# One core: the first step written out apart, odd experts' weights a step later, two reorderings at layer one's opening and tail, and the first pair's down projection a step nearer

## The chip, the core and the metric

The kernel runs on one core of one Trainium2 chip, in one launch. The core's engines run their own instruction lists side by side and meet at semaphores: PE (TensorE, matrix products and transposes), DVE (VectorE), ACT (ScalarE), POOL (GpSimd) and SP (SyncE, which here only issues DMAs). The metric is the device time of one launch in microseconds (us), the median of several runs.

## The reference

Eight sequences of 1024 tokens of 128 features go through a sparse feed-forward layer, a linear attention and the same feed-forward layer again:

```
x = x + 0.5 * ffn(layernorm(x))
x = x + attn(layernorm(x))        # elu+1 features, 16 heads of 8, kv = k^T v, then q kv
x = x + 0.5 * ffn(layernorm(x))
...
logits = xf @ gate_w + gate_b                       # 16 experts
top_vals, top_idx = top_k(softmax(logits), 2)       # two experts a token
y = sum over the two of  w * ((silu(x @ w1 + b1) * (x @ w3 + b3)) @ w2 + b2)
z = (silu(x @ sw1 + sb1) * (x @ sw3 + sb3)) @ sw2 + sb2     # shared, inner width 352
ffn = y + z
```

## The kernel before

There are 64 tiles of 128 tokens, in 8 groups of 8 tiles (a group is one sequence) and 16 chunks of 4 tiles. Five phases follow each other, with a barrier of all engines between them: `front(0)`, `experts(0)`, `front(1)`, `experts(1)`, `combine`.

**front(n)** normalizes the tokens, computes gate logits, picks two experts a token, gives each token a slot in its expert's region of a table `xs` in the chip's main memory, and sends each row there: 128 rows (a tile) an indirect DMA, one for the first choice and one for the second, 128 sends a phase, issued by POOL in a fixed order (`first(c)`, `second_choice(c)` for chunk c, four sends each). It also computes the shared feed-forward (`ups`, `silus`, `gates`, `downs`, `outs`). `front(1)` reads the experts' results, computes the attention as well, and prepares the same for the second feed-forward.

Each engine's program is a list written out by hand. DVE's, ACT's and PE's lists are made of steps s = 1 to 9 (`step(s)`), and a step works on three things at once: routing of group s (`largest`, `indices`, `hot`, `sums`, `places` on DVE; `gating_mm`, `count` on PE), statistics of group s + 2 (`moments`, `variances`, `scales`), and the shared feed-forward of group s - 1, in six pieces m = 6(s-1) to 6(s-1)+5 (two chunks of three feature blocks; `gates(m)` on DVE needs `silus(m)` of ACT, which needs `ups(m)` of PE). `places(s)` writes the slots that POOL's `first(2s)` and `first(2s+1)` wait for.

A row of `xrow` carries a token with its destination and weight. The second choice reuses the same buffer: **`rewrite(c)`** on DVE writes destination and weight of the second choice over those of the first, and so must wait until the four first sends of chunk c have landed (its wait on `sent0`); POOL's `second_choice(c)` waits for it. An instruction that waits holds up everything that stands behind it on its engine.

In layer 0 the 16 experts' first-layer weights are centred as well, one expert at a time, two a step: `weight_mean(e)` on PE, `weight_high(e)` on ACT (`w13h`), `weight_low(e)` on DVE (`w13l`, L642). Before the change expert 2s and 2s+1 belong to step s, the odd one at its end.

ACT's DMA queue loads all eight groups of x. SP's queue loads gate and shared weights, experts 0 to 3, then fills the table's padding rows (`xs<-zero`, 2 MB, and `xs<-pad_tail`, 8 bytes a row), then `w2` and the rest.

**experts(n)** goes over 72 pairs of 128-row tiles of `xs`. PE's step j does `x` transposes of pair j+1 (`px`, L1498), products with w1 and w3 of the pair j+1 or j (`pu`, L1509 to L1511), transposes of the activated product (`pa`, L1521) and, from j = 2 on, the down projection of pair j-2 (`py`, L1534). ACT copies `pa` to `at` (L1471). DVE multiplies (`a`) and scales the result (`y`, L1446), and POOL sends two tiles a pair to `ys` (L1415).

Of the kernel before, what the change touches and what calls it, by code (L numbers as in the profile page):

```python
# [139 lines left out]
def front(nc, k, sb, ps, n, xa, xs, w=None, ys=None):  # L140

    with phase(nc) as sem, ExitStack() as ctx:
# [33 lines left out]
        if n == 0:  # L176
            raw13 = [t(f"raw13{r}", [P, UP]) for r in range(4)]
            rawb = [t(f"rawb{r}", [P, UP]) for r in range(4)]
            raws = t("raws", [P, 2 * SH])
            k.centre, k.part = t("centre", [P, P]), t("part", [P, P])  # L180
            rawq, rowq = t("rawq", [P, 3 * D]), t("rowq", [P, 3 * D])
            rawp = t("rawp", [33, D])
# [47 lines left out]

        def turn_of(g, h=None):

            return g + 1 if h is None else h
# [5 lines left out]
        with nc.Block(no_gpsimd_drain=True) as block:  # L239
            @block.sync  # L240
            def _(sp):
                if n == 0:
# [26 lines left out]
                    load_expert(3)  # L269
                    sp.wait_ge(tail, 2)  # L270
# [142 lines left out]
            def _(dve):  # L413
# [269 lines left out]
                def step(s):  # L683
                    m, new, gating = 6 * (s - 1), s + 2 < GROUPS, 0 <= s < GROUPS
                    if 0 <= s < GROUPS - 1:
# [24 lines left out]
                    outs(2 * (s - 1))  # L710
                    if gating:
                        places(s)
                    if s == GROUPS - 1:
                        tables()
                    gates(m + 5)
                    if s > 1:
                        rewrite(2 * (s - 1) + 1)
                    if gating:
                        if n == 0:
                            weight_low(2 * s)  # L720
                        low(2 * s)
                        low(2 * s + 1)
                        if n == 0:
                            weight_low(2 * s + 1)
# [128 lines left out]
                if n == 0:  # L853
                    for r in range(4):
                        dve.memset(rawb[r][:], 0.0)
                    dve.memset(k.w2[0:32, 1], 0.0)
                    dve.memset(rawp[:], 0.0)
                    dve.memset(rowq[:], 0.0).then_inc(zeroed, 1)
                    moments(0)
                    variances(0)  # L860
                    scales(0)
                    shifts(0)
                    moments(1)
                    variances(1)
                    scales(1)
                for r in range(2):
                    dve.memset(gated[r][96:97, 2], 1.0)
# [31 lines left out]
            def _(act):  # L899
                if n == 0:  # L900
                    for g in range(GROUPS):
                        act.dma_start(xa[:, of(g)],
                                      w["x"][:, ds(g, 1)].rearrange("p b i d -> p (b i) d")
                                      ).then_inc(x_in[g], 16)
# [49 lines left out]
                def step(s):  # L954
# [4 lines left out]
                    silus(m + 1)  # L959
                    silus(m + 2)  # L960
# [11 lines left out]
                    if gating:  # L972
                        high(2 * s + 1)
                        if n == 0:
                            weight_high(2 * s + 1)
# [46 lines left out]
                def opening():  # L1022
# [12 lines left out]
                    rows_a(4)  # L1035
                    exps(0)
                    rows_a(5)
                    turned_a(4)
                    high(0)
                    turned_a(5)  # L1040
# [41 lines left out]
                if n == 0:  # L1082
                    step(-1)
                    step(0)
                    act.wait_ge(sw_in, 32)
                    act.activation(k.sw13h[:], raws[:], ACT.Copy).then_inc(swhi, 1)
                    act.wait_ge(share_in, 16 * 9)
# [13 lines left out]
            def _(pe):  # L1101
# [87 lines left out]
                def step(s):  # L1189
                    gating = 0 <= s < GROUPS  # L1190
                    for i in range(6):
# [3 lines left out]
                        ups(m)  # L1195
                        downs(m - 2)
# [8 lines left out]
                        if i == 5:  # L1205
                            turn(2 * s + 3)
                            if gating and n == 0:
                                weight_mean(2 * s + 1)
# [96 lines left out]
                def step_1(s):  # L1305
# [9 lines left out]
                    for i in range(6):  # L1315
# [4 lines left out]
                        if i == (1 if s == 1 else 0) and gating:  # L1320
# [10 lines left out]
                if n == 0:  # L1331
                    pe.wait_ge(consts, 3)
                    step(-1)
                    pe.wait_ge(centre, 1)
                    step(0)
# [17 lines left out]
def experts(nc, k, sb, ps, n, xs, ys):  # L1353


    with phase(nc) as sem, ExitStack() as ctx:
# [31 lines left out]
        with nc.Block(no_gpsimd_drain=True) as block:  # L1388
# [34 lines left out]
            def _(dve):  # L1423
# [4 lines left out]
                def step(j, jv):  # L1428
# [12 lines left out]
                    if 2 <= j:  # L1441
                        s = (j - 2) % RING
                        dve.wait_ge(down, jv - 1)
                        dve.sem_inc(passed, 1)
                        for t in range(2):
                            last = dve.tensor_scalar(  # L1446
                                y[s][:, t], p_y[j % 2][:, t * D:(t + 1) * D],
                                xin[s][:, t, D + 1:D + 2], None, ALU.mult)
                        last.then_inc(yy, 1)
# [25 lines left out]
            def _(pe):  # L1475
# [14 lines left out]
                def step(j, jv):  # L1490
# [33 lines left out]
                    if 2 <= j:  # L1524
                        r = j % 2
                        pe.wait_ge(turned, jv - 1)
                        wait(pe, yy, jv - 3)
                        for t in range(2):

                            for c, rows_ in enumerate((A0 + 1, A0)):  # L1530
                                q = slice((2 * t + c) * P, (2 * t + c + 1) * P)
                                w2 = k.w2[0:rows_, c, ds(expert[j - 2][t], 1)].rearrange(
                                    "p e n -> p (e n)")
                                last = pe.matmul(p_y[r][:, t * D:(t + 1) * D], at[r][0:rows_, q],  # L1534
                                                 w2, start=c == 0, stop=c == 1,
                                                 skip_group_check=True)
                        last.then_inc(down, 1)
# [70 lines left out]
```

## Time and profile before

| | us |
|---|---|
| median of 3 runs (lowest to highest) | 942.99 (941.9 to 943.26) |
| the profiled execution, its own time | 942.32 |
| span of its trace | 940.6 |
| POOL busy, share of the span | 568.9, 60% |
| PE busy | 785.1, 83% |
| DVE busy | 580.3, 62% |
| ACT busy | 470.5, 50% |
| front(0): POOL's last send starts | 211.02 |
| experts(0): POOL's first and last send start | 229.18, 414.58 |
| front(1): DVE's last `outs` starts | 700.72 |
| experts(1): POOL's first send starts | 717.48 |

Times of the trace are counted from the start of the span; the engine that is busiest over the whole span is not the one that ends each phase, so the phases are read one by one. POOL's busy time is that of issuing sends; between two sends in a row it has a short gap that the profile puts down to "issue".

### The profile page before, as it was taken

The numbers are of one execution on the slowest core, as the hardware profiler recorded it, in microseconds if no ns is written. First come the engines' busy times: TensorE is split into PE (matmuls) and PEld (weight loads), VectorE is DVE, ScalarE is ACT, GpSimd is POOL, SyncE is SP. The second block draws the span as 40 slices with busy tenths as digits, with TensorE's granted clock in tenths as the row PEclk, the third lists the DMA queues.
The fourth block names the chain that finished last, engine by engine and source line by source line (L and its number), as shares of the span: only waits on it lengthen the run. The fifth ranks groups of instructions, "written<-read, shape, count | busy, mean of one in ns | idle before, by whom it ended". The sixth has DMA issues, their size and how long they took to land. (4 is left out here: it accounts for less than half of the span.)

```text
span 940.6 us, 20435 instructions
## 1 busy us (share of the span) xinstructions
PE 785.1 (83%) x5348; PEld 699.7 (74%) x5349; DVE 580.3 (62%) x2146; ACT 470.5 (50%) x968; POOL 568.9 (60%) x585
## 2 busy tenths in 40 slices
PE   2899999886999999936678999999868999999910
PEld 2577777666999999934567777787758999999900
DVE  7688786643555555537667877766634555555535
ACT  2465566423555555525457667675314555555500
POOL 1376777772777776751167667765643777776730
PEclk9999999997999999977889999999798999999965
DMA  9921221132333333324112211111133333333349
GB/s 279 157 65 55 70 70 59 52 98 66 102 101 101 104 101 101 100 97 145 65 32 83 76 39 46 35 38 35 43 81 81 108 101 104 101 101 98 93 185 376
DMA packets 83816, 90.45 MB, mean 96 GB/s; under 512 B 20391, under 2 KB 69421, under 8 KB 82733
## 3 DMA queue, kind: packets, MB, share of 16 engines
q1 hardware_dynamic: 64046, 45.41, 19.1%
q0 software_dynamic: 17408, 35.95, 11.4%
q10 hardware_dynamic: 2304, 8.39, 2.3%
q8 instruction: 27, 0.44, 0.2%
q14 instruction: 31, 0.25, 0.1%
HBM read 47.45 MB, written 44.37 MB: 98 GB/s over the span
## 5 line engine op out<-in xcount | busy, mean ns | idle before, releaser
L1415 POOL DMA_INDIRECT ys<-e_y,e_x x288 | 276.6, 960 | 134.4 <-issue 88.7
L354 POOL DMA_INDIRECT xs<-f_xrow,f_slot x256 | 261.1, 1020 | 128.0 <-issue 74.6
L1534 PE MATMUL e_py<-w,e_at 97*128 (+1 forms) x1152 | 152.1, 274 | 0.0
L1534 PEld LDWEIGHTS e_py<-w,e_at 97*128 97x128 f32 (+1 forms) x1152 | 139.9, 191 | 0.1
L1439 DVE TENSOR_TENSOR e_a<-e_pu,e_sil 128x352 f32<-128x352 f32 x144 | 75.6, 525 | 97.6 <-ACT e_sil L1465 97.6
L1446 DVE TENSOR_SCALAR e_y<-e_py,e_x 128x128 f32<-128x128 f32 x288 | 87.8, 347 | 57.6 <-PE e_py L1534 57.3
L1168 PEld LDWEIGHTS f_pz<-sw,f_gated 128*128 128x128 f32 (+1 forms) x768 | 101.6, 195 | 14.3 <-DVE f_gated L561 4.5
L1465 ACT ACTIVATE e_sil<-e_pu 128x352 f32<-128x352 f32 x144 | 67.0, 465 | 90.3 <-PE e_pu L1511 90.3
L1509 PE MATMUL e_pu<-w13h,e_xth 128*128 x288 | 107.2, 372 | 0.0
L1459 ACT ACTIVATE e_xth<-e_px 128x256 fp32r<-128x256 f32 x144 | 55.6, 386 | 101.0 <-PE e_px L1498 101.0
L1168 PE MATMUL f_pz<-sw,f_gated 128*128 128x128 f32 (+1 forms) x768 | 103.4, 279 | 3.0 <-DVE xa L571 2.9
L946 ACT ACTIVATE f_sil<-f_phg,sb 128x512 f32<-128x512 f32 (+1 forms) x96 | 65.3, 686 | 78.9 <-PE f_phg L1154 74.7
L561 DVE SCALAR_TENSOR_TENSOR f_gated<-f_phg,sb,f_sil 128x512 f32<-128x512 f32 (+1 forms) x96 | 71.5, 746 | 41.2 <-ACT f_sil L946 35.6
L1154 PE MATMUL f_phg<-f_xth,sw13h 128*128 128x512 f32 (+1 forms) x192 | 88.1, 459 | 8.4 <-ACT f_sil L946 6.4
L1510 PE MATMUL e_pu<-w13l,e_xth 128*128 x288 | 94.3, 327 | 0.0
L1511 PE MATMUL e_pu<-w13h,e_xtl 128*128 x288 | 94.2, 327 | 0.0
L1471 ACT ACTIVATE e_at<-e_pa 96x512 f32<-96x512 f32 x144 | 85.8, 596 | 1.6 <-PE e_pa L1521 1.6
L1521 PE MATMUL e_pa<-ident,e_a 128*96 128x128 f32 x576 | 86.2, 272 | 0.0
L1154 PE MATMUL f_phg<-f_xtl,sw13h 128*128 128x512 f32 (+1 forms) x192 | 77.6, 404 | 0.0
L1154 PE MATMUL f_phg<-f_xth,sw13l 128*128 128x512 f32 (+1 forms) x192 | 77.6, 404 | 0.0
L1498 PE MATMUL e_px<-ident,e_x 128*128 128x128 f32 x288 | 57.7, 282 | 21.2 <-DMA e_x<-xs 17.0
L1521 PEld LDWEIGHTS e_pa<-ident,e_a 128*96 128x96 f32 x576 | 67.2, 125 | 5.1
(168 smaller groups left out, 1320.2 us busy)
## 6 DMA issues: line engine op xcount, KB each, us to landing
e_x<-xs SPq DMA_DIRECT2D x288, 65.0 KB
f_yt<-ys SPq DMA_DIRECT2D x16, 512.0 KB, 4.1
c_yt<-ys SPq DMA_DIRECT2D x8, 1024.0 KB, 10.4
ys<-e_y,e_x POOLq DMA_INDIRECT x288
xa<-in_attn_x ACTq DMA_DIRECT2D x8, 512.0 KB, 9.8
xs<-f_xrow,f_slot POOLq DMA_INDIRECT x256, 2.4
out<-xa ACTq DMA_DIRECT2D x8, 512.0 KB
f_raw<-in_ffn_w SPq DMA_DIRECT2D x32, 88.0 KB
```

The costliest lines, as they stand in the source:

```text
L354: pool.indirect_dma_start(xs, bass.IndirectOffsetOnAxis(slot[:, q, i:i + 1], 0), xrow[:, i, :], None).then_inc(done, 16)
L1154: last = pe.matmul(p_hg[(2 * m + g) % NH][0:wd], w_[:, cols], x_[c % NX][:], start=q == 0, stop=q == 2)
L1168: last = pe.matmul(p_z[c % NZ][:, tok], gated[c % 2][0:wd, f, tok], k.sw2[0:wd, f], start=f == 0 and q == 0, stop=f == 2, skip_group_check ...
L1415: pool.indirect_dma_start(ys, bass.IndirectOffsetOnAxis(xin[r][:, t, D:D + 1].bitcast(I32), 0), y[r][:, t, :], None).then_inc(sent[r], 16)
L1439: dve.tensor_tensor(a[r][:], p_u[r][:, :, INTER:UP], sil[r][:], ALU.mult).then_inc(aa, 1)
L1446: last = dve.tensor_scalar(y[s][:, t], p_y[j % 2][:, t * D:(t + 1) * D], xin[s][:, t, D + 1:D + 2], None, ALU.mult)
L1471: act.activation(at[r][0:A0], p_a[0:A0], ACT.Copy).then_inc(turned, 1)
L1509: pe.matmul(o, xth[r][:, tok], k.w13h[:, cols], start=True, stop=False)
L1510: pe.matmul(o, xth[r][:, tok], k.w13l[:, cols], start=False, stop=False)
L1511: last = pe.matmul(o, xtl[r][:, tok], k.w13h[:, cols], start=False, stop=True)
L1521: last = pe.transpose(p_a[0:A0, q * P:(q + 1) * P], a[r][:, t, o:o + A0], k.ident[:])
L1534: last = pe.matmul(p_y[r][:, t * D:(t + 1) * D], at[r][0:rows_, q], w2, start=c == 0, stop=c == 1, skip_group_check=True)
```

## The change

Five edits, all of order:

1. Loads: ACT's queue loads groups 0 to 2 of x, and groups 3 to 7 go on SP's queue after expert 3 and ahead of the padding. ACT runs one Exp on a constant before it starts.
2. The first step of layer 0 is written out by itself. DVE does the whole routing of group 0, `low(0)`, `low(1)`, the split of the shared weights (`sw13l`) and `weight_low(0)`, and only then the statistics of group 2. ACT interleaves rows and transposed copies by chunk. PE transposes group 1 before it counts group 0.
3. In all steps `rewrite(2(s-1))`, and in step 1 `rewrite(1)`, come directly behind `gates(m)`. The odd expert's three weight operations go from the end of step s to the start of step s+1.
4. `front(1)`: DVE computes both `phi_k` pieces before `shifts` and `shifts_a`; ACT's opening puts rows and transposes ahead of `exps(0)`; in step 7 PE counts (`count(7)`) behind `ups(37)` and `downs(35)` and no longer in front of them.
5. `experts`: the down projection of pair 0 and its scaling are done in step j = 1, directly behind the `pa` transposes of the same pair; step 2 has none, and from j = 3 on all is as before.

```diff
@@ front, SP's list
                     load_expert(2)
                     load_expert(3)
+                    for g in range(3, GROUPS):
+                        load_tokens(sp, g)
                     sp.wait_ge(tail, 2)
...
@@ front, DVE's step(s)
                     gates(m)
                     if s == GROUPS:
                         tables_out()
-                    gates(m + 1)
-                    outs(2 * (s - 1) - 1)
                     rewrite(2 * (s - 1))
-                    gates(m + 2)
                     if s == 1:
                         rewrite(1)
+                    gates(m + 1)
+                    if s <= GROUPS:
+                        weight_low(2 * s - 1)
+                    outs(2 * (s - 1) - 1)
+                    gates(m + 2)
...
                 def features(a):
                     phi_q(a, 0)
                     phi_q(a, 1)
+                    phi_k(a, 0)
+                    phi_k(a, 1)
                     shifts(a - 1)
                     shifts_a(a + 1)
-                    phi_k(a, 0)
-                    phi_k(a, 1)
...
@@ front, DVE, layer 0
                 if n == 0:
-                    step(0)
+                    largest(0)
+                    indices(0)
+                    hot(0)
+                    sums(0)
+                    places(0)
+                    low(0)
+                    low(1)
                     dve.wait_ge(swhi, 1)
                     dve.tensor_tensor(k.sw13l[:], raws[:], k.sw13h[:].bitcast(F32), ALU.subtract
                                       ).then_inc(swlo, 1)
+                    weight_low(0)
+                    moments(2)
+                    variances(2)
+                    scales(2)
...
@@ front, PE's step(s) of layer 0, and of layer 1
                         ups(m)
+                        if i == 1 and n == 0 and s <= GROUPS:
+                            weight_mean(2 * s - 1)
                         downs(m - 2)
...
-                        if i == (1 if s == 1 else 0) and gating:
+                        if i == (1 if s in (1, GROUPS - 1) else 0) and gating:
                             count(s)
...
@@ experts, PE (DVE's weigh alike)
+                    if j == 1:
+                        down_projection(2, 2)
+                    if j > 2:
+                        down_projection(j, jv)
```

DVE's list, front of layer 0, first step with feed-forward (`phg` is the product that `gates` takes up, `xrow<-rec,wtop` and `xrow<-dest1` are one `rewrite`); before:

```order
L561 SCALAR_TENSOR_TENSOR f0_gated0<-f0_phg1,sb13,f0_sil0 128x512
L561 SCALAR_TENSOR_TENSOR f0_gated0<-f0_phg0,sb13,f0_sil1 128x512
L542 SCALAR_TENSOR_TENSOR f0_xrow<-f0_rec,f0_wtop 128x4
L544 COPY f0_xrow<-f0_dest1 128x4
L561 SCALAR_TENSOR_TENSOR f0_gated0<-f0_phg2,sb13,f0_sil0 96x512
L542 SCALAR_TENSOR_TENSOR f0_xrow<-f0_rec,f0_wtop 128x4
L544 COPY f0_xrow<-f0_dest1 128x4
```

The same place after the change:

```order
L568 SCALAR_TENSOR_TENSOR f0_gated0<-f0_phg1,sb13,f0_sil0 128x512
L549 SCALAR_TENSOR_TENSOR f0_xrow<-f0_rec,f0_wtop 128x4
L551 COPY f0_xrow<-f0_dest1 128x4
L549 SCALAR_TENSOR_TENSOR f0_xrow<-f0_rec,f0_wtop 128x4
L551 COPY f0_xrow<-f0_dest1 128x4
L568 SCALAR_TENSOR_TENSOR f0_gated0<-f0_phg0,sb13,f0_sil1 128x512
L649 TENSOR_TENSOR w13l<-f0_pw,w13h 128x352
L568 SCALAR_TENSOR_TENSOR f0_gated0<-f0_phg2,sb13,f0_sil0 96x512
```

Both rewrites stand now ahead of the second and third `gates`, and one `weight_low` has come in between those.

PE's list, experts of layer 0, second half of step 1 and start of the next; before:

```order
L1521 MATMUL e0_pa<-ident,e0_a0 96x128 x4
L1498 MATMUL e0_px<-ident,e0_x3 128x128 x2
L1509 REGISTER_ALU
L1509 ISA
L1509 MATMUL e0_pu0<-w13h,e0_xth0 128x352
```

After the change:

```order
L1557 MATMUL e0_pa<-ident,e0_a0 96x128 x4
L1575 ISA
L1575 MATMUL e0_py0<-w2,e0_at0 128x128
L1575 ISA
L1575 MATMUL e0_py0<-w2,e0_at0 128x128
L1575 ISA
L1575 MATMUL e0_py0<-w2,e0_at0 128x128
L1575 ISA
L1575 MATMUL e0_py0<-w2,e0_at0 128x128
L1534 MATMUL e0_px<-ident,e0_x3 128x128 x2
```

The four products of the down projection, which need ACT's copy `at0` of the `pa` just made, stand now in front of the transposes of pair 3.

## Rows read from the trace of the kernel before

**Rows 1.** The page: transfer rate in 40 slices, a DMA queue, an instruction group, a DMA issue.
```profile
GB/s 279 157 65 55 70 70 59 52 98 66 102 101 101 104 101 101 100 97 145 65 32 83 76 39 46 35 38 35 43 81 81 108 101 104 101 101 98 93 185 376
...
q0 software_dynamic: 17408, 35.95, 11.4%
...
L561 DVE SCALAR_TENSOR_TENSOR f_gated<-f_phg,sb,f_sil 128x512 f32<-128x512 f32 (+1 forms) x96 | 71.5, 746 | 41.2 <-ACT f_sil L946 35.6
...
xs<-f_xrow,f_slot POOLq DMA_INDIRECT x256, 2.4
```

**Rows 2.** Waits of POOL, 100.5 to 212: waited for, total us, times, longest.
```profile
POOL xs L354 <- issue: 24.4, 80, 0.3
```

**Rows 3.** Timeline of POOL, front(0): start, duration, instruction, [idle before it <- releaser].
```profile
31.55 1.12 POOL L354 DMA_INDIRECT xs<-f_xrow,f_slot  x1 [27.35 <-DVE f_slot L532]
46.44 0.96 POOL L354 DMA_INDIRECT xs<-f_xrow,f_slot  x1 [4.50 <-DVE f_xrow L544]
...
57.07 2.04 POOL L354 DMA_INDIRECT xs<-f_xrow,f_slot  x1 [0.82 <-DVE f_slot L532]
...
78.32 2.46 POOL L354 DMA_INDIRECT xs<-f_xrow,f_slot  x1 [5.29 <-DVE f_slot L532]
...
100.57 2.21 POOL L354 DMA_INDIRECT xs<-f_xrow,f_slot  x1 [0.82 <-DVE f_slot L532]
```

**Rows 4.** Timeline of DVE, front(0).
```profile
29.15 0.28 DVE L516 TENSOR_TENSOR f_spot<-f_pg,f_base 128x128 f32<-128x128 f32 x1
...
46.87 0.15 DVE L542 SCALAR_TENSOR_TENSOR f_xrow<-f_rec,f_wtop 128x4 f32<-128x4 f32 x1
...
55.81 0.42 DVE L532 CAST f_slot<-f_at 128x16 int32<-128x16 f32 x1
...
59.18 0.53 DVE L642 TENSOR_TENSOR w13l<-f_pw,w13h 128x352 fp32r<-128x352 f32 x1 [0.91 <-ACT w13h L951]
```

**Rows 5.** Timeline of PE, front(0).
```profile
24.55 0.69 PE L1121 MATMUL f_pg<-f_mask,onesb 128*128 128x128 bf16 x8
...
36.00 3.59 PE L1108 MATMUL f_pg<-gw_s,f_xt 128*128 128x16 f32 x16 [2.16 <-DVE sw13l L885]
```

**Rows 6.** Timeline of SP's queue, front(0).
```profile
18.27 7.26 SPq L274 DMA_DIRECT2D xs<-pad_tail  x1
```

**Rows 7.** DMA view, 31 to 44: queue, packets, MB, share of 16 engines.
```profile
q0 software_dynamic: 184, 0.40, 11.4%
```

**Rows 8.** Waits of POOL, 233 to 416, experts(0).
```profile
POOL ys L1415 <- issue: 44.5, 136, 1.9
```

**Rows 9.** Timeline of all engines, experts(0), first pairs.
```profile
224.92 0.38 PE L1498 MATMUL e_px<-ident,e_x 128*128 128x128 f32 x2
...
225.12 0.59 ACT L1471 ACTIVATE e_at<-e_pa 96x512 f32<-96x512 f32 x1
...
226.56 1.06 PE L1534 MATMUL e_py<-w,e_at 97*128 x8
...
234.60 0.96 POOL L1415 DMA_INDIRECT ys<-e_y,e_x  x1 [0.67 <-issue]
```

**Rows 10.** Timeline of all engines, opening of front(1).
```profile
454.54 0.17 DVE L611 SCALAR_TENSOR_TENSOR f_nma<-f_mva,f_rsa 128x8 f32<-128x8 f32 x1 [1.29 <-POOL f_rsa L381]
...
455.09 1.22 PE L1246 MATMUL f_pb<-f_phk,f_v 128*128 128x128 f32 x4 [4.51 <-DVE f_phk L622]
```

**Rows 11.** Timeline of all engines, tail of front(1).
```profile
665.90 0.29 PE L1118 MATMUL f_pg<-f_mask,tri 128*128 128x128 bf16 x1 [2.00 <-DVE f_mask L504]
...
669.23 1.91 PE L1168 MATMUL f_pz<-sw,f_gated 97*128 97x128 f32 x8
...
672.22 0.24 DVE L516 TENSOR_TENSOR f_spot<-f_pg,f_base 128x128 f32<-128x128 f32 x1
...
674.45 0.96 POOL L354 DMA_INDIRECT xs<-f_xrow,f_slot  x1 [2.60 <-DVE f_slot L532]
...
688.60 0.17 DVE L542 SCALAR_TENSOR_TENSOR f_xrow<-f_rec,f_wtop 128x4 f32<-128x4 f32 x1 [5.62 <-DMA xs<-f_xrow,f_slot]
```

More of the change, by code:

```diff
@@ L712, in step @@
                         places(s)
+                    gates(m + 5)
+                    if gating:
+                        weight_low(2 * s)
+                        low(2 * s)
+                        low(2 * s + 1)
                     if s == GROUPS - 1:
                         tables()
-                    gates(m + 5)
                     if s > 1:
                         rewrite(2 * (s - 1) + 1)
[L718 to L724, printed above, removed]
                 def features(a):
@@ L865, in _ @@
                     scales(1)
+                    shifts(1)
                 for r in range(2):
@@ L900, in _ @@
                 if n == 0:
[L901 to L904, printed above, removed]
+                    for g in range(3):
+                        load_tokens(act, g)
+                    act.wait_ge(tail, 1)
+                    act.activation(primed[:], k.ones_e[:, 0:1], ACT.Exp)
                 def rows(c):
@@ L959, in step @@
                     silus(m + 1)
+                    if n == 0:
+                        weight_high(2 * s - 1)
                     silus(m + 2)
@@ L1082, in _ @@
                 if n == 0:
-                    step(-1)
-                    step(0)
+                    for c in range(2):
+                        rows(c)
+                        turned(c)
+                    rows(2)
+                    rows(3)
+                    turned(2)
+                    exps(0)
+                    turned(3)
+                    high(0)
+                    high(1)
                     act.wait_ge(sw_in, 32)
                     act.activation(k.sw13h[:], raws[:], ACT.Copy).then_inc(swhi, 1)
+                    weight_high(0)
                     act.wait_ge(share_in, 16 * 9)
@@ L1332, in _ @@
                     pe.wait_ge(consts, 3)
-                    step(-1)
+                    turn(0)
+                    turn(1)
+                    gating_mm(0)
+                    turn(2)
+                    turn(3)
+                    count(0)
                     pe.wait_ge(centre, 1)
-                    step(0)
+                    weight_mean(0)
                     pe.wait_ge(swlo, 1)
@@ L1440, in step, with weigh @@
                                           ).then_inc(aa, 1)
[L1441 to L1449, printed above, removed]
+                    if j == 1:
+                        weigh(2, 2)
+                    if j > 2:
+                        weigh(j, jv)
+                def weigh(j, jv):
+                    s = (j - 2) % RING
+                    dve.wait_ge(down, jv - 1)
+                    dve.sem_inc(passed, 1)
+                    for t in range(2):
+                        last = dve.tensor_scalar(
+                            y[s][:, t], p_y[j % 2][:, t * D:(t + 1) * D],
+                            xin[s][:, t, D + 1:D + 2], None, ALU.mult)
+                    last.then_inc(yy, 1)
                 steps(dve, step, PAIRS + 2)
@@ L1523, in step, with down_projection @@
                         last.then_inc(apose, 1)
[L1524 to L1537, printed above, removed]
+                    if j == 1:
+                        down_projection(2, 2)
+                    if j > 2:
+                        down_projection(j, jv)
+                def down_projection(j, jv):
+                    r = j % 2
+                    pe.wait_ge(turned, jv - 1)
+                    wait(pe, yy, jv - 3)
+                    for t in range(2):
+                        for c, rows_ in enumerate((A0 + 1, A0)):
+                            q = slice((2 * t + c) * P, (2 * t + c + 1) * P)
+                            w2 = k.w2[0:rows_, c, ds(expert[j - 2][t], 1)].rearrange(
+                                "p e n -> p (e n)")
+                            last = pe.matmul(p_y[r][:, t * D:(t + 1) * D], at[r][0:rows_, q],
+                                             w2, start=c == 0, stop=c == 1,
+                                             skip_group_check=True)
+                    last.then_inc(down, 1)
                 load_experts(0, list(range(HEAD)))
```

17 lines of the change are left out of this document (8 added, 9 removed).

## The prediction

> **What bounds the kernel now.** The busiest engine over the span is PE, yet each phase is ended by something else, so I first read the waits of POOL inside a phase. From 100.5 on in front(0), and from 233 on in experts(0), nearly all of them are "issue", a gap of 24.4/80 = 0.305 us and 44.5/136 = 0.327 us between two sends [rows 2, 8]: POOL always has a send ready and these stretches are paced by it. A usual send takes 0.96, so with its gap 1.265 us. There a cut on PE or DVE is worth nothing; a shift is worth something only where POOL still waits for somebody, which is in four places: ahead of its first sends of groups 0 to 2 and the second choices between them [rows 3], at the first pairs of each experts phase [rows 9], in the opening of front(1) [rows 10] and at its tail [rows 11]. The change touches all four.
>
> **Front(0), first sends.** POOL's first send starts at 31.55, having waited for the slots [rows 3]. The chain into the slots starts with `spot` at 29.15; PE had finished the count it reads at 24.55 + 0.69 = 25.24 [rows 4, 5]. Between stood the statistics of group 2 on DVE, which the change puts behind. So `spot` moves by 29.15 - 25.24 = 3.9 and the first send to 27.7. The Exp table is loaded earlier too, but ACT now alternates rows and copies; I put that at nothing net, 1 us either way.
>
> **Front(0), the rewrites.** The eighth first send ended at 46.44 - 4.50 = 41.94 [rows 3]; now 38.1. `rewrite(0)` and `rewrite(1)` wait for these sends to land. Before, `rewrite(1)` stood behind three `gates` and ran at 46.87 without a listed idle time [rows 4], so its sends had landed. When? A send is 17408/544 = 32 packets (544 sends: 256 here, 288 of the experts) [rows 1]; eight are 256, and by 44 only 184 were through [rows 7]. So the landing came between 44 and 46.87, 2.1 to 4.9 us behind the last send's end; the usual landing is 2.4 us after issue [rows 1]. Now `rewrite(1)` stands ahead of `gates(1)`, and what is queued behind it on DVE is `gates(1)`, a `weight_low`, `gates(2)`, `hot(1)` and so on to `places(1)`, for which POOL's next first sends wait. The sends also meet other traffic: the 2.6 MB of x that ACT's queue had loaded now go ahead of the padding on SP's queue. At the page's 279 GB/s [rows 1] they take 9.4 us, and the padding, whose 8-byte rows SP needed 7.26 us merely to issue [rows 6], shifts by up to that and lies over the landing of the eighth send. I take a lag of 6 us, a little over the upper bound of before: `rewrite(1)` at T = 44.1. Bounds: 2.1 us (T = 40.2), and 12 us (T = 50), the lag with most of the 9.4 on top.
>
> Is DVE ready by then? `rewrite(1)` ran at 46.87 [rows 4]. The statistics' 3.9 are gone from ahead of it, so is PE's wait of 2.16 for `sw13l` at the step's start, 36.00 [rows 5], since that split is moved up as well, and two `gates` of 0.75 [rows 1] stand behind it: 46.87 - 3.9 - 2.16 - 1.5 = 39.3, ahead of both bounds. So the landing decides, not the gates.
>
> From `rewrite(1)` to the end of the slot cast it took 55.81 + 0.42 - 46.87 = 9.4 [rows 4]. Now two more `gates` (746 ns each [rows 1]) and one `weight_low` (0.53 [rows 4]) lie behind it, less a little overlap: 11.2, plus 0.3 for both rewrites. Slots of group 1: 44.1 + 11.5 = 55.6 where they were at 56.2, **-0.6**. Group 1 to group 2 takes 78.32 - 57.07 = 21.25 [rows 3] and I leave it: the odd weight saves its wait of 0.9 at the step's end [rows 4] and spends it in the middle of the next. From group 2 to 3 it takes 100.57 - 78.32 = 22.25 [rows 3], while 16 sends at 1.265 with one long one (2.46 instead of 0.96 [rows 3]) need 21.7, or 21.3 with the shorter of the long ones; the rest, about **-0.75**, goes, since `rewrite` runs sooner in every step. From there POOL is gapless in both. Sum -1.4; it is T - 45.45. Bounds -5.3 and +4.6.
>
> A rule of the Trainium skill bears on the lag ("DMA: Bandwidth & Descriptors", section "Queues, rings and completion order"): a DMA engine goes round between the queues it has work for and changes after each packet. By that rule the sends would not stand behind the whole padding, and would land near the usual time. In the trace the eighth send's lag of 2.1 to 4.9 us, beside padding and w2 traffic, fits the rule only in part: it is the usual time or twice that [rows 1, 3, 7].
>
> **Front(1), opening.** DVE's `phi_k` stood behind `shifts_a`, whose instruction at 454.54 idled 1.29 us for POOL's result and took 0.17; PE waited 4.51 us for `phi_k` [rows 10]. With `phi_k` first, PE goes on 1.29 + 0.17 = **1.45** sooner, and what follows moves with it. The rows that wait for `shifts` come two `phi_k` later, which ACT's time can cover. Bounds 0 and -1.5.
>
> **Front(1), tail.** PE stood still 2.00 us for the mask ahead of the count at 665.90 [rows 11], with `ups(37)` and `downs(35)` behind it. Done first, from 663.9, these take 669.23 - 665.90 - 0.78 = 2.55 and 1.91 [rows 11], so the count ends at 663.9 + 4.5 + 0.8 = 669.2, and `gates(37)` and `outs(11)` on DVE, which stood ahead of `spot`, are done by then as well. `spot`, at 672.22, moves to 669.2; POOL's send started 2.23 behind it [rows 11], so it could start at 671.4. POOL is free and past its usual gap of 0.3 at 674.45 - 2.60 + 0.3 = 672.15 [rows 11]. So its 2.60 of idle time shrinks to 0.3: **-2.3**. The last stall, a rewrite that waits 5.62 for landing [rows 11], follows POOL and moves along. Bounds 0 and -2.3.
>
> **Experts.** PE came to the place of the new `down(0)` right after the `pa` transposes, when it went on with `px` at 224.92. The product needs ACT's `at0`, which ran from 225.12 to 225.71 [rows 9]. So PE now stands until 225.7 and computes for 0.9 (the block took 1.06 with its last end [rows 9]): `px` of pair 3 starts at 226.6, 1.7 later. The old place, 226.56, then is empty and gives 0.9 back. Net 0.75 to 0.8 late for everything from pair 2 on. The first send comes 0.9 sooner, but POOL sent pair 2 at 234.60 after 0.67 instead of 0.3 [rows 9]: it had waited already, so the later `y` delays it, and from there it is gapless to the end [rows 8]. Hence **+0.75** in each of two phases, +1.5. Bounds for each +0.9, and -0.9 if the pairs behind catch up, so that POOL's earlier start counts.
>
> **Sum**, against the profiled execution's 942.32: -1.4 - 1.45 - 2.3 + 1.5 = -3.65, so 938.7. The median of the runs is 942.99, 0.7 above that execution; no change would be 941.1 to 944.9, the 0.2% that a measurement of this kernel can just tell. All of front(0) hangs on T: the total is 894.6 + T.
>
> **Rivals.**
> - *The sends land at the usual pace* (T = 40.2): 942.32 - 5.3 - 1.45 - 2.3 + 1.5 = 934.8. For it: the lag of 2.1 that the rows allow, and the rate of other traffic that the sends outlived before. Against: no send before had 2.6 MB more ahead of the padding. Chance 0.2. The round between queues that the Trainium skill states ("DMA: Bandwidth & Descriptors") would make this the likelier one; the trace bears it out in part.
> - *The sends land late and DVE stands* (T of 50.3 or more): from 944.9 up, slower. For it: `rewrite(1)` now blocks DVE and with it everything to `places(1)`, where before it had three `gates` as cover. Against: it needs a lag of 12 us, more than twice any that the rows allow. At 46.5 to 50.3 it eats the gains and the time is the same. Chance of slower by it 0.15.
> - *The earlier down projection gains* (-0.9 a phase): 942.32 - 1.4 - 1.45 - 2.3 - 1.8 = 935.4. Against: POOL's wait at pair 2. Chance 0.1.
> - *The gains don't reach the end* (opening and tail of front(1) hidden behind other waits, front(0) as computed): 942.32 - 1.4 + 1.5 = 942.4, no change. For it: the opening is a chain of several engines, and the gap at 674.45 is one of a list. Chance 0.15.
>
> **How the numbers follow.** My forecast, with T between 42 and 46.5, has 0.4 and gives 936.6 to 941.1. Cases that are faster: forecast, usual pace, experts' gain, less the edges: 0.62. Same: hidden gains and T of 46.5 to 50.3: 0.23. Slower: 0.15. The full bounds are 942.32 - 5.3 - 1.5 - 2.3 - 1.8 = 931.4 and 942.32 + 4.6 + 1.8 = 948.7; leaving a tenth out on either side I give 934 to 944.8.
>
> **What would show it.** In the profile after: POOL's first send at 27.7; `rewrite(1)` on DVE at 44 with an idle time put down to the DMA of `xs`; the first sends of groups 1, 2, 3 at 56.5, 77.7 and 99.2; in experts(0) the first send 0.9 earlier against the phase's first load, and at pair 2 a POOL wait of about 2.3 us (0.67 + 0.75 + 0.9); in front(1) PE's wait for `phi_k` down to 3.0, and the last group's first send after 0.3 instead of 2.60 of idle time. I am wrong if `rewrite(1)` comes before 41 or behind 50, if another engine takes over as the one that holds `places(1)` (the count on PE, say), or if POOL's 2.60 goes and comes back in the stall of 5.62.

## The result and the profile after

| | before | after |
|---|---|---|
| median of 20 runs (lowest to highest), us | 942.61 (937.51 to 945.49) | 946.22 (941.83 to 950.35) |
| profiled execution, own time | 942.32 | 949.66 |

The ratio is 1.0039, 95% interval 1.0026 to 1.0052: slower by 0.4%, and the median of after lies above the forecast range (934 to 944.8). The profiled execution of after lies near the top of its runs, so the ledger below shows where the time went, with too large a sum: 7.3 us where the medians differ by 3.6.

From the timelines of POOL, with each phase's sends marked by the start of the first and the last one:

| stretch, us | before | after | difference | forecast |
|---|---|---|---|---|
| start to last send of front(0) | 211.02 | 217.95 | +6.9 | -1.4 |
| from there to last send of experts(0) | 203.56 | 205.36 | +1.8 | +0.75 |
| from there to last send of front(1) | 280.92 | 278.05 | -2.9 | -3.75 |
| from there to last send of experts(1) | 207.44 | 208.93 | +1.5 | +0.75 |

The loss is made in front(0). The timeline of DVE there, after the change:

```profile
25.29 0.29 DVE L523 TENSOR_TENSOR f_spot<-f_pg,f_base 128x128 f32<-128x128 f32 x1 [0.43 <-PE f_pg L1147]
...
38.01 0.75 DVE L568 SCALAR_TENSOR_TENSOR f_gated<-f_phg,sb,f_sil 128x512 f32<-128x512 f32 x1 [1.01 <-ACT f_sil L963]
44.59 0.17 DVE L549 SCALAR_TENSOR_TENSOR f_xrow<-f_rec,f_wtop 128x4 f32<-128x4 f32 x1 [5.82 <-DMA xs<-f_xrow,f_slot]
...
50.16 0.17 DVE L549 SCALAR_TENSOR_TENSOR f_xrow<-f_rec,f_wtop 128x4 f32<-128x4 f32 x1 [5.33 <-DMA xs<-f_xrow,f_slot]
...
59.71 0.75 DVE L568 SCALAR_TENSOR_TENSOR f_gated<-f_phg,sb,f_sil 128x512 f32<-128x512 f32 x1 [1.35 <-ACT f_sil L963]
...
62.39 0.17 DVE L539 CAST f_slot<-f_at 128x16 int32<-128x16 f32 x1
```

`spot` follows PE at once, at 25.29 instead of 29.15 [rows 4]. DVE is ready for `rewrite(0)` at 38.8 and then stands twice for the landing of the sends, 5.82 and 5.33 us. `rewrite(1)` runs at 50.16, 3.3 later than before although everything ahead of it came earlier, and the slots of group 1 end at 62.56 instead of 56.23. POOL, the same stretch:

```profile
27.70 1.22 POOL L361 DMA_INDIRECT xs<-f_xrow,f_slot  x1 [23.51 <-DVE f_slot L539]
...
45.65 0.95 POOL L361 DMA_INDIRECT xs<-f_xrow,f_slot  x1 [7.90 <-DVE f_xrow L551]
...
63.41 1.23 POOL L361 DMA_INDIRECT xs<-f_xrow,f_slot  x1 [7.45 <-DVE f_slot L539]
...
85.32 1.09 POOL L361 DMA_INDIRECT xs<-f_xrow,f_slot  x1 [6.36 <-DVE f_slot L539]
...
107.60 1.09 POOL L361 DMA_INDIRECT xs<-f_xrow,f_slot  x1 [2.21 <-DVE f_slot L539]
```

Against [rows 3] the first send is 3.85 earlier and the first of groups 1, 2 and 3 are 6.3, 7.0 and 7.0 later. The eighth send ended at 45.65 - 7.90 = 37.75 and had landed by 50.16: a lag of 12.4 us. What ran beside the sends at that time shows in the DMA view from 36 to 40 (queue, packets, MB, share of 16 engines), after:

```profile
q0 software_dynamic: 79, 0.18, 78.6%
q1 hardware_dynamic: 1650, 0.01, 70.8%
```

and before:

```profile
q1 hardware_dynamic: 1396, 0.71, 79.2%
q0 software_dynamic: 69, 0.14, 9.9%
```

q0 carries the sends. After the change 79 of its packets took 78.6% of 16 engines for 4 us, 0.786 x 16 x 4 / 79 = 0.64 us each, and before 0.09 us each. Beside them q1 had 1650 packets that make up 0.01 MB: the 8-byte rows of the padding. (The shares of the two queues add up to 149%, so packets of both overlap, and the 0.64 holds some of the other queue's time.)

While DVE stands, `gates(1)` behind the rewrites stands too, and PE waits for their result. The timeline of PE after the change, and the view by stretches (start and end, length, busy time and instructions of PE, PEld, DVE, ACT and POOL, granted clock of PE, DMA share, GB/s):

```profile
51.20 0.76 PE L1180 MATMUL f_phg<-f_xth,sw13h 128*128 128x512 f32 x1 [8.74 <-DVE f_gated L568]
51.77 0.63 PE L1180 MATMUL f_phg<-f_xtl,sw13h 128*128 128x512 f32 x1
...
46.00:50.00 4.00, 0.00 (x0) 0.00 (x0) 0.00 (x0) 0.00 (x0) 3.08 (x4) 0.64 1.19 203
50.00:54.00 4.00, 2.80 (x7) 2.25 (x8) 3.81 (x15) 1.14 (x3) 2.55 (x4) 0.50 1.02 242
54.00:58.00 4.00, 4.00 (x23) 3.38 (x21) 3.55 (x24) 1.08 (x3) 1.66 (x2) 0.58 0.24 80
```

PE idled 8.74 us, from 42.46 on. From 50 to 54 the granted clock was 0.50, the 1.2 GHz level, and the products start about 0.43 us apart. In the version below with only the 8-byte rows late, PE has work at that time:

```profile
50.00:54.00 4.00, 4.00 (x30) 3.41 (x29) 3.69 (x16) 3.48 (x9) 1.80 (x2) 1.00 1.04 85
```

There the clock is 1.00 and such products start 0.23 apart. After the change DVE then waits 1.35 at 59.71 for ACT's `sil`, which hangs on the slow products.

In the experts' phase, the timeline of all engines around the early down projection:

```profile
232.02 0.59 ACT L1507 ACTIVATE e_at<-e_pa 96x512 f32<-96x512 f32 x1
...
232.75 1.15 PE L1575 MATMUL e_py<-w,e_at 97*128 x8 [0.77 <-ACT e_at L1507]
...
233.74 0.38 PE L1534 MATMUL e_px<-ident,e_x 128*128 128x128 f32 x2
...
235.47 0.96 POOL L1446 DMA_INDIRECT ys<-e_y,e_x  x1 [16.57 <-DVE e_y L1482]
...
238.81 0.43 PE L1534 MATMUL e_px<-ident,e_x 128*128 128x128 f32 x2 [0.70 <-issue]
...
239.66 0.96 POOL L1446 DMA_INDIRECT ys<-e_y,e_x  x1 [1.97 <-DVE e_y L1482]
...
243.26 0.96 POOL L1446 DMA_INDIRECT ys<-e_y,e_x  x1 [1.38 <-DVE e_y L1482]
```

PE waits 0.77 for `at0`, as worked out, and at 238.81 another 0.70 that the trace of before does not list; POOL then waits at the second and third pair, 1.97 and 1.38, where it had waited 0.67 once [rows 9]. In front(1), PE's wait for `phi_k` and the last rewrite's wait:

```profile
463.12 0.89 PE L1272 MATMUL f_pb<-f_phk,f_v 128*128 128x128 f32 x4 [3.01 <-DVE f_phk L629]
...
694.10 0.17 DVE L549 SCALAR_TENSOR_TENSOR f_xrow<-f_rec,f_wtop 128x4 f32<-128x4 f32 x1 [5.24 <-DMA xs<-f_xrow,f_slot]
```

The first fell from 4.51 to 3.01 [rows 10], the second stayed nearly as it was, 5.24 after 5.62 [rows 11], and POOL no longer waits for the last group's slots.

### The profile page after: what moved, and what is told of

Same layout as the page of the kernel before. It is cut to its first block and busy times, and to the rows that moved or that the text cites. A ratio compares the mean times of both kernels' runs of the same rounds, so it can differ in the third digit from the quotient of the medians.

```text
span 947.8 us, 20437 instructions
## 1 busy us (share of the span) xinstructions
PE 793.5 (84%) x5348; PEld 706.1 (74%) x5349; DVE 580.0 (61%) x2146; ACT 469.6 (50%) x969; POOL 561.7 (59%) x585
## 5 line engine op out<-in xcount | busy, mean ns | idle before, releaser
L361 POOL DMA_INDIRECT xs<-f_xrow,f_slot x256 | 254.7, 995 | 138.1 <-issue 73.7
L1194 PEld LDWEIGHTS f_pz<-sw,f_gated 128*128 128x128 f32 (+1 forms) x768 | 103.8, 199 | 16.0 <-DVE f_gated L568 4.4
L1194 PE MATMUL f_pz<-sw,f_gated 128*128 128x128 f32 (+1 forms) x768 | 105.6, 283 | 3.7 <-DVE xa L578 3.6
```

The source lines that it names most:

```text
L361: pool.indirect_dma_start(xs, bass.IndirectOffsetOnAxis(slot[:, q, i:i + 1], 0), xrow[:, i, :], None).then_inc(done, 16)
L1194: last = pe.matmul(p_z[c % NZ][:, tok], gated[c % 2][0:wd, f, tok], k.sw2[0:wd, f], start=f == 0 and q == 0, stop=f == 2, skip_group_check ...
```

## The experiments

Ratios are to the kernel before in runs on the same chip, with a 95% interval. Positions are from each one's profiled execution, in us; T is the start of `rewrite(1)`. In the kernel before it waits for no landing; in after it does, so the two values of T have different causes.

| kernel | ratio | T | first send of groups 1, 2, 3 | front(0), last send |
|---|---|---|---|---|
| before | 1 | 46.87 | 57.07, 78.32, 100.57 | 211.02 |
| after | 1.0039 (1.0026 to 1.0052) | 50.16 | 63.41, 85.32, 107.60 | 217.95 |
| x back on ACT's queue | 1.0000 (0.9977 to 1.0022) | 46.89 | 58.85, 81.14, 103.03 | 212.97 |
| 8-byte rows late | 0.9959 (0.9939 to 0.9978) | 43.43 | 55.23, 75.79, 97.39 | 208.21 |
| whole padding late | 1.0009 (0.9991 to 1.0027) | 46.51 | 58.30, 80.58, 102.50 | 213.16 |
| rewrites back | 0.9985 (0.9964 to 1.0005) | 48.64 | 59.40, 81.66, 103.59 | 213.57 |
| experts back | 0.9978 (0.9953 to 1.0002) | 49.27 | 62.21, 84.51, 106.58 | 217.05 |
| before, 8-byte rows late | 1.0006 (0.9989 to 1.0023) | 48.60 | 58.53, 79.97, 102.20 | 212.39 |
| rows late, experts back | 0.9932 (0.9910 to 0.9954) | 43.89 | 55.57, 76.54, 98.42 | 209.06 |
| the same, rewrites back | 0.9913 (0.9891 to 0.9935) | 44.27 | 54.21, 75.54, 97.20 | 207.31 |

**The x loads back on ACT's queue** (all else as changed):

```diff
-                    for g in range(3, GROUPS):
-                        load_tokens(sp, g)
...
-                    for g in range(3):
+                    for g in range(GROUPS):
                         load_tokens(act, g)
```

> The changed kernel with all eight x loads back on ACT's queue; all else as changed. Theory (the padding's 8-byte rows, pushed behind x on SP's queue, meet the first eight sends and make them land late): the padding is through early again, the eighth send lands 2 to 6 us after its end, rewrite(1) runs at 41 to 44.5 instead of 50.2, the first send of group 1 at 54 to 56 instead of 63.4, and the time falls by 5 to 8 against the changed kernel, ratio to before 0.994 to 0.998. Rival (the place of the x loads does not matter, the sends are late because they start 4 us sooner into the same traffic): rewrite(1) stays at 48 or later, ratio 1.002 to 1.005.

Measured: T = 46.89 and a ratio of 1.0000, both between the two theories. The padding rows were issued at 18.22 as before, yet the sends, 3.85 us earlier than before, still ran into them: from 33 to 38 the queue's packets took 0.734 x 16 x 5 / 104 = 0.56 us each.

```profile
q0 software_dynamic: 104, 0.23, 73.4%
q1 hardware_dynamic: 681, 0.06, 47.3%
```

So the place of the x loads is worth 3.3 of T (1.8 and 2.4 against the other two kernels with the same loads, which had 48.64 and 49.27). The rest of the collision stays with the x loads back, where the sends' earlier start is enough for it.

**Only the 8-byte rows late:**

```diff
-                    sp.dma_start(rows[:, :, D:ROW], k.pad_tail[:]).then_inc(padded, 16)
...
                     for dst, part in rest:
                         sp.dma_start(dst, part).then_inc(rest_in, 16)
+                    sp.dma_start(rows[:, :, D:ROW], k.pad_tail[:]).then_inc(padded, 16)
```

> The changed kernel, with only the DMA of the padding's 8-byte rows moved behind w2 and the other weights on SP's queue; the 2 MB zero fill stays. Theory (the 8-byte rows make the sends slow): each packet of the sends' queue takes a few tenths less time between 36 and 44, rewrite(1) runs at 42 to 45, ratio 0.994 to 0.998. Rival (any traffic of that size holds the sends: the zero fill, or w2 that now takes the place): rewrite(1) at 48 or later, ratio 1.001 to 1.005.

Measured: T = 43.43, ratio 0.9959, as the theory expected. Timeline of DVE, and DMA view, 36 to 40:

```profile
43.43 0.17 DVE L549 SCALAR_TENSOR_TENSOR f_xrow<-f_rec,f_wtop 128x4 f32<-128x4 f32 x1 [1.96 <-DMA xs<-f_xrow,f_slot]
...
q1 hardware_dynamic: 1318, 0.67, 90.8%
q0 software_dynamic: 98, 0.21, 24.9%
```

A send's packet now takes 0.249 x 16 x 4 / 98 = 0.16 us, though the other queue moves 0.67 MB in the same time instead of 0.01. It is the many small rows, not the bytes, that hold the sends. In the profiles the front ends 9.7 us earlier than in that of after.

**The whole padding late** (the zero fill too, moved behind the weights):

```diff
-                    sp.dma_start(rows[:, :, 0:D], k.zero[:].unsqueeze(1).to_broadcast(
-                        [P, PADS, D])).then_inc(padded, 16)
-                    sp.dma_start(rows[:, :, D:ROW], k.pad_tail[:]).then_inc(padded, 16)
...
                         sp.dma_start(dst, part).then_inc(rest_in, 16)
+                    sp.dma_start(rows[:, :, 0:D], k.zero[:].unsqueeze(1).to_broadcast(
+                        [P, PADS, D])).then_inc(padded, 16)
+                    sp.dma_start(rows[:, :, D:ROW], k.pad_tail[:]).then_inc(padded, 16)
```

> The changed kernel with the whole padding, the 2 MB zero fill and the 8-byte rows, behind w2 and the other weights on SP's queue. If only the 8-byte rows hold the sends, this is as with these rows alone moved: rewrite(1) at 43 to 44, the first send of group 1 at 55, ratio 0.994 to 0.998. If the zero fill held them too, rewrite(1) comes at 40.5 to 42 and the first send of group 1 at 53 to 54, ratio 0.992 to 0.996. If the fill now meets the sends of the second choices and makes them slow, group 2's first send is later than 75.8.

Neither of the first two came: `rewrite(0)` ran at 41.32, but T = 46.51 after a wait of 4.94, and the ratio is 1.0009. Group 2's first send was late, at 80.58, but by T already and not by the second choices. Without the fill ahead of them the weights are issued by 30.16 already, and the padding follows (timeline of SP's queue):

```profile
30.16 0.41 SPq L293 DMA_DIRECT2D xs<-zero  x1
30.61 8.38 SPq L295 DMA_DIRECT2D xs<-pad_tail  x1
```

So the rows are issued from 30.61 on, where the version above issues them at 43.75, and from 42 to 46 q1 has 3349 packets, over the landing of the eighth send (DMA view, 42 to 46):

```profile
q1 hardware_dynamic: 3349, 0.17, 142.7%
q0 software_dynamic: 54, 0.11, 18.5%
```

This run also answers whether it is the table, and not the size of the rows, that the sends share with the padding. The fill goes to the same table, and by the order of the list it is what the queue moves just ahead of the rows; from 36 to 40:

```profile
q1 hardware_dynamic: 1367, 0.70, 98.5%
q0 software_dynamic: 79, 0.18, 19.3%
```

Beside it a send's packet takes 0.193 x 16 x 4 / 79 = 0.16 us, as beside the weights. What counts is when the rows run, not their place in the list.

**The rewrites of step 1 back behind the gates:**

```diff
-                    rewrite(2 * (s - 1))
-                    if s == 1:
-                        rewrite(1)
+                    if s > 1:
+                        rewrite(2 * (s - 1))
                     gates(m + 1)
                     if s <= GROUPS:
                         weight_low(2 * s - 1)
                     outs(2 * (s - 1) - 1)
+                    if s == 1:
+                        rewrite(0)
                     gates(m + 2)
+                    if s == 1:
+                        rewrite(1)
```

> The changed kernel with the two rewrites of step 1 back behind the second and third gates; later steps as changed. Theory (the landing sets T, the order of rewrites only what stands behind it): rewrite(1) still at about 50, two gates and one weight less behind it, the first send of group 1 about 2 us sooner at 61.5, ratio 1.001 to 1.003. Rival (the waiting rewrite itself is what costs): rewrite(1) waits little or nothing and the first send of group 1 is at 57 or sooner, ratio 0.996 to 0.999.

T = 48.64 after a wait of 3.75 for the sends, so the landing is still what sets it; the way from there to the first send of group 1 fell from 13.25 to 10.76, and the front ends 4.4 earlier. The mechanism of the theory holds: the landing sets T, and the gates queued behind the waiting rewrite cost 2.5 on top. Its sizes do not: the first send of group 1 came at 59.40 instead of 61.5, and the ratio, 0.9985, is below its range and within the rival's.

**The experts' phases as before:**

```diff
-                    if j == 1:
-                        down_projection(2, 2)
-                    if j > 2:
+                    if 2 <= j:
                         down_projection(j, jv)
```

(and DVE's scaling alike.)

> The changed kernel with the experts' phases as before (down projection of pair 0 in step 2). Theory (the early projection costs PE and the register loads behind it; sends behind pair 2 are gapless): each phase 1.5 to 1.8 us shorter, 3.3 in sum, ratio 1.0000 to 1.0010. Rival (the experts' phases are hidden or gain from it): no change against the changed kernel, ratio 1.003 to 1.005.

The experts' sends take 185.25 and 185.43 us from first to last, as before, instead of 187.84 and 187.77. Over the profiles the stretch from front(0)'s last send to that of experts(0) is 203.0 to 204.0 in the eight kernels with the projection as before and 205.0 to 206.0 in the five with it early, means 203.5 and 205.5; for layer one, in kernels with the count moved, the means are 208.6 (five) and 209.7 (five). So +2.0 and +1.1; in layer one the two sets overlap (208.0 to 209.9 and 208.9 to 210.7). The ratio fell by 0.006, some 5.8 us, to 0.9978, below the expected 1.0000 to 1.0010. That is more than the 3.1 of the profiles, which lies at the edge of what the two intervals, 0.0026 and 0.0049 in width, leave open; the two ratios also come from different runs of before.

**The kernel before with late rows** (the same move of one line as above, in the kernel before):

> The kernel before with only the 8-byte padding rows behind the weights. Before, these rows were through by about 33, ahead of nearly all of the sends' packets: if so, nothing is to be gained, ratio 0.999 to 1.001, front(0)'s last send at 210 to 211.5, and the rows now fall among the sends of the second choices. Rival (late rows are good in themselves, and the change's first step brings nothing): front(0) ends 2 to 3 sooner, ratio 0.996 to 0.998.

No gain, 1.0006: before, the sends began at 31.55 and the rows were nearly through. With the rows later, T is even 1.7 later, after a wait of 1.32 for the sends, and the front ends at 212.39, beyond the expected 211.5. The two edits pay only together: the early first step with the rows in their place costs 2.0 us of front(0) (the version with x back, which has the moved rewrites too), the late rows alone bring nothing, both give 2.8 (2.0 in the version below, whose front is the same).

**Late rows and the experts as before:**

> The changed kernel with the 8-byte padding rows behind the weights and the experts' phases as before. Theory (front(0) wins 2.8 once the rows are out of the way, front(1) wins 2.9 to 3.9, the experts' phases are as before): 5.7 to 6.7 us below before, ratio 0.993 to 0.994. Rival (the gain of either was chance of a run): ratio above 0.9965.

0.9932, in the expected range; by the medians, 936.82 against 941.97 on that chip, it is 5.2 us or 0.9945, a little less than the 5.7 to 6.7 expected and still within the interval. **The same with the rewrites of step 1 back:**

> As the one with late rows and the experts as before, and with step 1's rewrites back behind the second and third gates. If DVE's wait of 4.4 us for the landing is what delays group 1's slots, the gates fill it and the first send of group 1 comes 1 to 2 us sooner, at 53.5 to 54.2, and the front ends 1 to 2 sooner; ratio 0.991 to 0.993. If POOL is the limit by then (16 sends from 27.7 on and the second choices from 42 on, about 53), less than 1.

0.9913, 934.28 us: faster than both kernels. Its timeline of DVE:

```profile
42.25 0.16 DVE L549 SCALAR_TENSOR_TENSOR f_xrow<-f_rec,f_wtop 128x4 f32<-128x4 f32 x1
44.27 0.17 DVE L549 SCALAR_TENSOR_TENSOR f_xrow<-f_rec,f_wtop 128x4 f32<-128x4 f32 x1 [0.17 <-DMA xs<-f_xrow,f_slot]
```

and of POOL:

```profile
54.21 1.06 POOL L361 DMA_INDIRECT xs<-f_xrow,f_slot  x1 [1.08 <-DVE f_slot L539]
```

DVE's waits of 2.2 and 2.7 us are filled with gates, the first send of group 1 comes 1.4 sooner and POOL waits 1.08 for it: 1.8 us at the front's end.

On this version four single edits were tried, on another chip than the one it had run on itself; its 0.9913 and theirs are each against the kernel before on their own chip. **The rows later still**, behind the load of expert 7:

> The best version so far (late 8-byte rows, experts as before, rewrites of step 1 back), with the rows later still, behind the load of expert 7. In the version above they are issued at about 43 and lie over the first second choices. If DVE's and POOL's path no longer touches them there: no change within 1 us, ratio 0.990 to 0.993. If the last of the eight sends still feels them: rewrite(1) earlier than 44.3 and the front 0.5 to 1.5 shorter. If they now slow sends that a rewrite waits for (between 60 and 80), the first send of group 2 comes later than 75.5.

0.9921 (0.9900 to 0.9942), the first sends of groups 2 and 3 at 75.27 and 97.16, within 0.3 of the version above: no difference in the front. **The count of step 7 back in front** (`1 if s == 1 else 0`):

> The best version so far, with the count of step 7 in layer 1 back in front of the feed-forward products. Theory (the tail's edit takes away POOL's wait of 2.60 ahead of the last group): that wait is back, front(1) from its first send to its last is 2 to 2.5 longer, ratio 0.993 to 0.994. Rival (it comes back in the last stall): the same length within 0.5, ratio as of the best version, 0.9913.

0.9956 (0.9940 to 0.9972), a larger loss than the 0.993 to 0.994 expected. POOL's timeline at the last group:

```profile
668.69 0.95 POOL L361 DMA_INDIRECT xs<-f_xrow,f_slot  x1 [1.84 <-DVE f_slot L539]
671.33 0.96 POOL L361 DMA_INDIRECT xs<-f_xrow,f_slot  x1 [1.69 <-issue]
```

Two waits are back, 1.84 and 1.69 instead of 0.3 each, and front(1) from its first to its last send takes 217.60 instead of 214.48: 3.1. Both had stood before as well, as 2.60 and 1.68; I had counted one. **The `phi_k` pieces back behind the shifts:**

> The best version so far, with layer 1's phi_k pieces back behind the shifts. Theory (PE waits 1.5 less at the opening and all behind it moves): the way from the experts' last send to front(1)'s first send is 1.4 longer, ratio 0.992 to 0.994. Rival (other waits hide it): no change, 0.9913.

0.9931 (0.9911 to 0.9951), which overlaps the version above, so the profiles must say. Starts of POOL's sends, counted from the last send of experts(0):

| kernel | send 1 | send 25 | send 33 | send 97 | first send of experts(1) |
|---|---|---|---|---|---|
| before | 63.8 | 103.0 | 119.0 | 236.7 | 302.9 |
| late rows, experts and rewrites back | 61.1 | 100.4 | 117.9 | 235.7 | 298.7 |
| with `phi_k` back | 63.9 | 103.0 | 119.0 | 236.8 | 299.3 |
| with the rows later | 62.1 | 101.2 | 118.9 | 236.7 | 299.9 |
| with the count back | 61.4 | 100.6 | 118.3 | 236.2 | 302.5 |

The opening is 1.8 to 2.8 sooner with `phi_k` first, and by the 33rd send 0.1 to 1.1 of that is left; the spread of these kernels among themselves is as large. Between the 32nd and the 33rd send POOL runs an instruction of its own, `rs`, which waits for DVE's `ve`; in the version with `phi_k` first, and with `phi_k` back:

```profile
524.83 1.67 POOL L368 TENSOR_TENSOR f_rs<-f_ve,nhalf 128x8 f32<-128x8 f32 x1 [4.22 <-DVE f_ve L447]
...
526.67 1.67 POOL L368 TENSOR_TENSOR f_rs<-f_ve,nhalf 128x8 f32<-128x8 f32 x1 [2.69 <-DVE f_ve L447]
```

In this pair POOL gives back 1.5 of its lead there. **The down projection of pair 0 ahead of the transposes of pair 1**, in step 2:

```diff
+                    if j == 2:
+                        down_projection(2, 2)
                     if 1 <= j < PAIRS + 1:
...
-                    if 2 <= j:
+                    if 2 < j:
                         down_projection(j, jv)
```

> The best version so far, with pair 0's down projection in step 2 ahead of the transposes of pair 1 instead of behind them, where ACT's copy is ready: PE waits for nothing, the first result comes 0.4 to 0.5 sooner, later pairs at the same time. Theory (pair 2's result sets the rest of the phase, POOL being gapless behind it): the first send 0.4 to 0.5 sooner, the last at the same time, from first to last 185.7 to 185.9, ratio unchanged at 0.9913. Rival (an earlier first result moves the whole chain of sends): from first to last 185.3 as now, each phase 0.4 to 0.5 shorter, ratio 0.990.

0.9927 (0.9907 to 0.9947); from first to last send 186.47 and 186.44 instead of 185.35 and 185.23, longer than either theory expected, and from the front's last send 204.67, 1.1 more than the mean above. An earlier first result brings nothing. Ahead of the later pairs PE has the same wait as in after, at the same place of the list; whether it is the whole loss is not shown:

```profile
228.00 0.43 PE L1535 MATMUL e_px<-ident,e_x 128*128 128x128 f32 x2 [0.72 <-issue]
```

At the opening of experts(0) this wait, 0.69 to 0.72, is listed in the five kernels with the early projection and in this one, and in none of the eight with the projection as before.

## Why the prediction was wrong

**The first sends** came at 27.70, as worked out, 3.85 earlier.

**The landing** is the step that failed: "I take a lag of 6 us". It was 12.4 in the profile of after, with T = 50.16 instead of 44.1; two other kernels with the same loads had 48.64 and 49.27. I had named the cause, the padding's small rows pushed over the landing by x, and had it as the upper bound of T and as a rival at 0.15, then taken a value "a little over the upper bound of before". That bound was read at a time when the rows were already through (0.09 us a packet), and so told nothing of a collision; the row with 184 packets and the issue time of 7.26 for the rows [rows 6, 7] were read as a delay, not as a price per packet. The experiments show both halves: 1.8 to 3.3 of T from the x loads' new place, the other part from the sends' own earlier start, all of it gone once the 8-byte rows run elsewhere. With these late, T was 43.4 to 43.9, near the 44.1 that I forecast; that is chance, since I meant this value for a kernel in which the rows lie over the landing.

The late landing is not the whole miss. By the forecast's own sum, 894.6 + T, a T of 50.16 gives 944.8, and the profile is 4.9 above that: 2.2 more in front(0), 1.8 in the experts' phases, 0.9 in front(1).

**What stands behind T** was sized at 11.5 up to the slots; it took 62.56 - 50.16 = 12.4. I had not counted that PE, too, would stand behind the blocked `gates`: its 8.74 us of idle time, the half clock behind it and DVE's wait of 1.35 at 59.71 are listed above. With the rows late and the clock at 1.00 the same way took 54.37 - 43.43 = 10.9. No run held the clock apart from the wait, so this share is read from the traces alone. **Groups 1 to 3**: 21.9 and 22.3 between the first sends instead of 21.25 and 21.5; with the rows late 20.6 and 21.6. Together some 2 us that I did not have in the profile of after.

**The rule on queues** says that a DMA engine goes round between its queues and changes after a packet (the Trainium skill, "DMA: Bandwidth & Descriptors", section "Queues, rings and completion order"). The trace agrees that the queues share: 79 packets of the one ran beside 1650 of the other. What failed is what I drew from the rule, a landing near the usual time; as I used it, it gave no time for a turn, and the sends took 0.64 us a packet and landed 12.4 us behind the end of their last issue.

**The experts' phases** had the right sign and half the size: +2.0 and +1.1, +3.1 in sum, for +1.5. Of what is missing in the first of them 0.7 is PE's new wait at 238.81, listed as "issue", which stands where the list loads the next pairs' expert numbers into registers; the forecast had nothing for it. That these loads are the cause is argued from the place in the list; no run took them away.

**The opening of front(1)**: PE's wait fell by 1.50 as computed (4.51 to 3.01), but the end did not move. From the last send of experts(0) to the first of experts(1) it takes 299.3 with `phi_k` back, and 298.7 to 299.9 in four kernels with it first, the experts as before and the count moved. The forecast's -1.45 is thus the rival "gains don't reach the end". The lead is given back around the 33rd send, where POOL's `rs` waits for DVE's `ve`. **The tail**: -2.3 forecast; 302.5 with the count back against that mean of 299.4, -3.1, since a second wait behind the first went too. In sum front(1) gave 3.5 of the 3.75 forecast in those four kernels, nearly all of it from the tail: the sum came out nearly right by luck, since one term fell out and the other was larger than computed.

In the ledger: +6.9 in front(0) for -1.4, and 1.8 more in the experts' phases, explain the sign; front(1) did nearly what was expected of it.

## What to carry to other kernels

When a chain is moved forward, look at what the DMA queues carry at its *new* time: a lag read at the old time is no bound for it. Thousands of rows of a few bytes are worth a place of their own in the schedule, where nothing waits for a landing. And a waiting instruction belongs behind the work that can cover its wait, as the gates did here: moved ahead of them, it adds them to the wait, and here it took the products from PE as well, whose clock then fell to half.

## What was unexpected of the hardware

The sends' packets took 0.64 us each beside the 8-byte rows, while the other queue moved 0.01 MB in 4 us, and 0.09 (before, 36 to 40) to 0.16 (rows late, and beside the zero fill) where it moved 0.67 to 0.71 MB. SP's issue of these rows took 7.26 us before [rows 6] and 11.50 behind x (below), but 0.41 where they were issued at 43.75; there the load behind them took 4.65.

```profile
17.34 0.52 SPq L279 DMA_DIRECT2D xs<-zero  x1
17.90 11.50 SPq L281 DMA_DIRECT2D xs<-pad_tail  x1
29.44 7.48 SPq L295 DMA_DIRECT2D w<-in_ffn_w  x1
```
